# Column mixing moved off the tensor engine, and a last batch in another order, in a decoder layer's attention stage

## The reference

```python
# attention: A has one value for each batch and column
Xn = layernorm(X) * gamma + beta
Q, K, V = split(Xn @ W_in + b_in, 3)
K, V = rotary(K, 256), rotary(V, 256)      # columns 2n and 2n+1 turn together
A = sum over tokens of (K / |K|) * (V / |V|)
A = 0.5 * A + 0.5
x1 = layernorm(X + (X + (A * Q) @ W_out + b_out))
# cross product: both sides rounded to an fp8 grid, scale = 448 / max|t| over the whole tensor
x2 = layernorm(x1 + q8(x1) @ q8(ctx) + mask)
# feed-forward: silu(x2 @ gate) * (x2 @ up) @ down, and 8 retrieved experts a token
out = layernorm(x2 + ffn(x2))
```

## Time and profile before

| | before |
|---|---|
| three runs | 790.91 us median (790.62 to 791.0) |
| the profiled execution: time, span | 791.2 us, 789.4 us |
| PE busy (share of the span) | 775.0 us (98%) |
| DVE | 664.5 us (84%) |
| POOL (GpSimd) | 360.5 us (46%) |
| ACT (ScalarE) | 322.0 us (41%) |
| mean granted TensorE clock | 0.997 |
| accumulating transfers `total<-prod` (384 KB) | 11, median 4.1 us to landing |
| accumulating transfers `xall<-half_bo` (1 MB) | 4, median 9.2 us to landing |

### The profile page before, as it was taken

The page is one execution under the profiler, slowest core; times in us unless marked ns, Lnnn a source line. Parts: engine busy times, 40 slices in busy tenths (PEclk is TensorE's granted clock), DMA queues, the critical chain, the costliest instruction groups (busy, mean ns, idle before and its releaser), DMA issues.

```text
span 789.4 us, 10701 instructions
## 1 busy us (share of the span) xinstructions
PE 775.0 (98%) x3586; PEld 637.9 (81%) x3590; DVE 664.5 (84%) x1348; ACT 322.0 (41%) x704; POOL 360.5 (46%) x313
## 2 busy tenths in 40 slices
PE   8999999999899999999999999999999999999997
PEld 7888888887678778888888888888888888888885
DVE  6888679998898871476779998999999999899876
ACT  5454336456574422223443433343333343344324
POOL 1241222232122411014476676775776677676324
PEclk9999999999999999999999999999999999999999
DMA  8656504624455629001122221331233323242014
GB/s 318 252 128 167 94 0 101 174 76 75 76 142 117 149 90 295 1 1 32 50 77 81 83 88 41 118 104 47 86 113 110 92 79 113 63 128 62 16 54 159
DMA packets 51334, 79.92 MB, mean 101 GB/s; under 512 B 17519, under 2 KB 26479, under 8 KB 50768
## 3 DMA queue, kind: packets, MB, share of 16 engines
q0 software_dynamic: 24240, 31.52, 19.1%
q1 hardware_dynamic: 25456, 47.72, 17.4%
q10 hardware_dynamic: 1584, 0.01, 0.1%
HBM read 110.64 MB, written 12.58 MB: 156 GB/s over the span
## 4 chain that ended last, share of the span: by engine, by line
PE 65%; DVE 3%; issue 2%; POOL 2%; ACT 1%; POOLq 0%; ACTq 0%; DVEq 0%
PE gu L1883 14%; PE gu L1884 14%; PE gu L1885 14%; PE ob L1957 6%; PE ob L1956 6%; PE ob L1961 6%; PE ob L1910 1%; POOL h_lo L1311 1%; DVE scratch L1575 1%; DVE x_lo L1622 1%; DVE scratch L1577 0%; PE gu L2055 0%; DVE xall L1616 0%; PE ob L1977 0%; POOL xall L153 0%
## 5 line engine op out<-in xcount | busy, mean ns | idle before, releaser
L1883 PE MATMUL gu<-x_hi,w_hi 128*128 128x512 f32 x516 | 201.4, 390 | 0.0
L1885 PE MATMUL gu<-x_hi,w_lo 128*128 128x512 f32 x516 | 200.8, 389 | 0.0
L1884 PE MATMUL gu<-x_lo,w_hi 128*128 128x512 f32 x516 | 200.7, 389 | 0.0
L1311 POOL TENSOR_TENSOR h_lo<-mid,h_hi 128x512 fp32r<-128x512 f32 x62 | 86.8, 1417 | 175.4 <-ACT h_hi L1461 175.4
L1885 PEld LDWEIGHTS gu<-x_hi,w_lo 128*128 128x128 f32 x516 | 96.8, 188 | 20.2
L1883 PEld LDWEIGHTS gu<-x_hi,w_hi 128*128 128x128 f32 x516 | 96.9, 188 | 20.0
L1884 PEld LDWEIGHTS gu<-x_lo,w_hi 128*128 128x128 f32 x516 | 96.9, 188 | 19.9
L1471 ACT ACTIVATE gates<-dots 128x1 f32<-128x1 f32 x144 | 29.2, 203 | 175.2 <-DVE dots L1724 175.2
L1633 DVE TENSOR_TENSOR mid<-gu,mid 128x512 f32<-128x512 f32 x64 | 44.0, 687 | 64.1 <-PE gu L1885 54.2
L1956 PE MATMUL ob<-w_hi,h_hi 128*128 128x512 f32 x224 | 87.1, 389 | 0.0
L1957 PE MATMUL ob<-w_lo,h_hi 128*128 128x512 f32 x224 | 87.1, 389 | 0.0
(11 more groups left out here) (254 smaller groups left out, 1438.1 us busy)
## 6 DMA issues: line engine op xcount, KB each, us to landing
stage<-in_ctx SPq DMA_DIRECT2D x7, 1024.0 KB, 5.8
total<-prod POOLq DMA_DIRECT2D x11, 384.0 KB, 4.1
xall<-half_bo POOLq DMA_DIRECT2D x4, 1024.0 KB, 9.2
xhat<-in_L_ffn_gate_w SPq DMA_DIRECT2D x8, 512.0 KB, 3.5
xhat<-in_L_ffn_up_w SPq DMA_DIRECT2D x8, 512.0 KB, 3.8
xall<-in_mask_Bx1xS_ff POOLq DMA_DIRECT2D x4, 1024.0 KB, 11.0
xhat<-in_L_ffn_down_w SPq DMA_DIRECT2D x8, 512.0 KB, 3.6
x_dram<-xall SPq DMA_DIRECT2D x4, 1024.0 KB, 7.8
```

The costliest lines, as they stand in the source:

```text
L1311: nc.gpsimd.tensor_tensor(lo[:, c], mid[c][:], hi[:, c].bitcast(F32), ALU.subtract).then_inc(hlo_done, 1)
L1883: nc.tensor.matmul(dst, lhs[0], rhs[0], start=start, stop=False)
L1884: nc.tensor.matmul(dst, lhs[0], rhs[1], start=False, stop=False)
L1885: return nc.tensor.matmul(dst, lhs[1], rhs[0], start=False, stop=stop)
```

## The change

1. **Mixing.** The products with `mix`, ScalarE's copy and the matrix itself are gone. The rotary columns of `total` are joined before the token sums, by three instructions of 128 x 256: on GpSimd for batches 0 to 2 (`mix_total`), on DVE for the last (in `last_total`). PE then sums four chunks, and `total` has two buffers, taken in turn.
2. **ctx.** The scale is made at the end of batch 1, and each rounding stands one place earlier: batch 3's in batch 2's first half, batch 0's at its end, batch 1's at the start of batch 3, batch 2's in its middle.
3. **Last batch.** All token sums stand together ahead of the last step of the third query chunk. The attention's first tile takes three chunks of y, then the fourth. The transposes of x1 stand behind the attention, and 16 idle products are gone.
4. **Variance.** For the last batch's tiles 0 to 2 DVE's residual also gives the row sums; ScalarE centres and squares, GpSimd makes the variance and the power. Batch 2's x1 is normalised by one ScalarE instruction a tile instead of two.
5. **Mask.** Batch 0's mask is added in two transfers of half the size, issued behind the last power.
6. **`low_ffn`** is on GpSimd, right behind the last bias transfer.

```diff
@@ GpSimd
-                    nc.gpsimd.dma_start(total[:], prod[:, i % 2], accum_op=ALU.add).then_inc(total_in, 16)
+                    nc.gpsimd.dma_start(totals[b % 2][:], prod[:, i % 2], accum_op=ALU.add).then_inc(total_in, 16)
+
+                def mix_total(b):
+
+                    pool.wait_ge(total_in, 16 * 3 * (b + 1))
+                    plain, turned = totals[b % 2][:, 0:ROT], totals[b % 2][:, D:D + ROT]
+                    apart = prod[:, 0, 0:ROT]
+                    own.did(nc.gpsimd.tensor_tensor(apart, plain, turned, ALU.subtract))
+                    own.did(nc.gpsimd.tensor_tensor(plain, plain, turned, ALU.add))
+                    own.wait()
+                    nc.gpsimd.tensor_tensor(plain.rearrange("p (n t) -> p n t", t=2), plain.rearrange("p (n t) -> p n t", t=2),
+                                            apart.rearrange("p (n t) -> p n t", t=2)[:, :, ::-1], ALU.add).then_inc(total_mixed, 1)
...
+                def low_ffn(s, part):
+                    pool.wait_ge(whi_done, s + 1)
+                    nc.gpsimd.tensor_tensor(part[1], w_stage[s].rearrange("p (c n) -> p c n", c=KC), part[0].bitcast(F32), ALU.subtract).then_inc(wlo_done, 1)
+
+                def last_rstd(i):
+
+                    pool.wait_ge(x1_scaled, i + 1)
+                    pool.wait_ge(last_squared, i + 1)
+                    own.did(nc.gpsimd.tensor_scalar(var2[:, i:i + 1], last_square[:, i:i + 1], 1.0 / D, LN_EPS, ALU.mult, ALU.add))
+                    own.wait()
+                    last_z_rstd(slice(i, i + 1))
+
+                for s, part in enumerate((gate_s[0], up_s[0])):
+                    low_ffn(s, part)
...
-                add_mask(0)
...
+                pool.wait_ge(x1_scaled, TB)
+                pool.wait_ge(var2_ready, LAST + 1)
+                last_z_rstd(slice(TB - 1, TB))
+                add_first_mask()
@@ ScalarE
-                def copy_sums(b):
...
+                def square_last(i):
+                    act.wait_ge(x1_centred, i + 1)
+                    if i:
+                        act.wait_ge(last_squared, i)
+                    nc.scalar.activation(junk[:], tile(TB * LAST + i), ACT.Square, accum_out=last_square[:, i:i + 1]).then_inc(last_squared, 1)
@@ DVE
-                    nc.vector.tensor_tensor(total[:], total[:], prod[:, (TB - 1) % 2], ALU.add).then_inc(total_all, 1)
+                    total = totals[LAST % 2]
+                    own.did(nc.vector.tensor_tensor(total[:], total[:], prod[:, (TB - 1) % 2], ALU.add))
+                    own.wait()
+                    plain, turned = total[:, 0:ROT], total[:, D:D + ROT]
+                    dve.wait_ge(total_mixed, LAST)
+                    apart = crossed[:]
+                    own.did(nc.vector.tensor_tensor(apart, plain, turned, ALU.subtract))
+                    own.did(nc.vector.tensor_tensor(plain, plain, turned, ALU.add))
+                    own.wait()
...
-                    if b == LAST:
-                        ctx_quantise(2)
+                    if b == LAST:
+                        ctx_quantise(3)
...
-                for s, part in enumerate((gate_s[0], up_s[0])):
-                    low_ffn(s, part)
@@ PE
-                        last = nc.tensor.matmul(ob[0][:, c:c + 1], total[:, c * P:(c + 1) * P], ones_col[:], start=(c == 0), stop=(c == CHUNKS - 1), skip_group_check=True)
+                        halved = 0 if c * P < ROT else 1
+                        last = nc.tensor.matmul(ob[0][:, c:c + 1], totals[b % 2][:, c * P:(c + 1) * P], sum_cols[:, halved:halved + 1], start=(c == 0), stop=(c == KC - 1), skip_group_check=True)
-                def mix_sums(b):
...
-                        for k in range(KC):
-                            pe.wait_ge(yhi_done, KC * b + k + 1)
...
+                        for chunks in (range(KC),) if b < LAST else (range(KC - 1), (KC - 1,)):
+                            for k in chunks:
+                                pe.wait_ge(yhi_done, KC * b + k + 1)
```

More of the change, by code:

```diff
@@ L132, in decoder_layer @@
         amax1 = keep("amax1", [P, 2], F32)
+        last_stats = keep("last_stats", [P, 4, TB], F32)
+        last_sum, last_minus, last_square, shift2 = (last_stats[:, i] for i in range(4))
         arow = keep("arow", [1, 4], F32)
@@ L154, in add_mask, with add_first_mask @@
                                 accum_op=ALU.add).then_inc(xm_in[b], 16)
+        def add_first_mask():
+            nc.gpsimd.wait_ge(x1t_mm, TB)
+            for first, landed in ((0, xm_in[0]), (2, xm_late)):
+                nc.gpsimd.dma_start(xall[:, first * D:(first + 2) * D].rearrange("p (t n) -> p t n", t=2), mask[0, 0].partition_broadcast(P).unsqueeze(1).broadcast_to([P, 2, D]),
+                                    accum_op=ALU.add).then_inc(landed, 16)
         s_const, ident_in = sem("s_const"), sem("ident_in")
@@ L177, in decoder_layer @@
             kv = sb("kv", [P, 2, 2, D], F32)
-            total = sb("total", [P, D + ROT], F32)
+            totals = [sb(f"total{i}", [P, D + ROT], F32) for i in range(2)]
             prod = sb("prod", [P, 2, D + ROT], F32)
@@ L364, in _ @@
                 last_z_rstd(slice(0, TB))
-                add_mask(0)
[L366 to L371, removed]
+                pool.wait_ge(minus_ready, 1)
+                pool.wait_ge(rstd2_ready, LAST)
+                nc.gpsimd.tensor_tensor(shift2, minus_m2[:], rstd2[:], ALU.mult).then_inc(shift_ready, 1)
+                for i in range(TB - 1):
+                    last_rstd(i)
+                pool.wait_ge(x1_scaled, TB)
+                pool.wait_ge(var2_ready, LAST + 1)
+                last_z_rstd(slice(TB - 1, TB))
+                add_first_mask()
+                first_psteps.append(own.base + own.n)
             @block.scalar
@@ L646, in products @@
                     k_t, v_t, w_t = kv[:, i % 2, 0], kv[:, i % 2, 1], wgt[:, i % 2]
-                    into = prod[:, i % 2] if i else total
+                    into = prod[:, i % 2] if i else totals[b % 2]
                     both, rotated, sinp = into[:, 0:D], into[:, D:D + ROT], crossed[:]
@@ L811, in _ @@
                     if b:
-                        for i in range(1, TB):
-                            residual(b - 1, i)
+                        residual(b - 1, 1)
+                        if b == 1:
+                            ctx_amax(3)
+                            dve.wait_ge(c_amax, B)
+                            largest(amax_c[:])
+                        residual(b - 1, 2)
+                        residual(b - 1, 3)
+                        if b == 1:
+                            scale_row()
                         variance(range(TB))
-                    if b == 1:
-                        ctx_amax(3)
-                        dve.wait_ge(c_amax, B)
-                        largest(amax_c[:])
+                        if b == 1:
+                            scale_all()
                 residual(LAST - 1, 0)
@@ L963, in query @@
                     for k in range(KC):
-                        if sums is not None and k:
-                            token_sums(sums, range(2 * k - 2, 2 * k))
-                        if mix_of is not None and k == 1:
-                            mix_sums(mix_of)
+                        if sums is not None and k == KC - 1:
+                            token_sums(sums, range(KC))
                         last = three(ob[2 + c % 2][:], w_hi[:, k, c * P:(c + 1) * P], w_lo[:, k, c * P:(c + 1) * P], xn_hi[:, k], xn_lo[:, k], k == 0, k == KC - 1)
@@ L1067, in _ @@
                 query(LAST, 2, sums=LAST)
-                query(LAST, 3, mix_of=LAST)
+                query(LAST, 3)
+                for i in range(TB):
+                    attention(LAST, i)
                 pe.wait_ge(x1_done, TB)
@@ L1074, in _ @@
                     last.then_inc(x1t_mm, 1)
-                for i in range(TB):
-                    attention(LAST, i)
                 def keep_running(count):
```

227 lines of the change are left out of this document (107 added, 120 removed).

## The result

The changed kernel takes 805.0 us (median of 4 runs, 804.6 to 805.9) against 790.95 us (4 runs, 790.62 to 791.53): a ratio of 1.0177 with a 95% interval of 1.0166 to 1.0189, so it is 14.1 us slower, where 792.9 (788.0 to 795.3) was forecast.

A forecast was written before the change was run, and what follows sets the result against it. PE was taken to set the time up to 205.0 us, DVE from there. Attention +1.0, tail -0.6 and clock +1.6 gave +2.0 on the median of 790.91: 792.9, range 788.0 to 795.3.

The forecast's parts named there:

- The mask: Start of the next stage: mask halves landing 6 and 11 to 12 us after issue cost 0, bounds 0 and 2.
- The rival about the mask: Next stage: the second mask half lands late, the third tile waits up to 2 us: 794.9; chance 0.14.
- The clock: Behind PE's 5.3 us stop before the last token sums: 3.4 us at 1.2 GHz, 1.7 lost at most, 1.6 taken.
- The first rival: PE's clock stays full through the stop before the last token sums: +0.4, 791.3; chance 0.28.
- The lower halves: Last batch's last products: GpSimd's two subtractions hold DVE for two turns, 4.7 us lost, bounds 0 and 4.8.
- A miss: GpSimd's subtractions hold DVE's last products once or not at all: 788.9 or 786.6; chance 0.16.
- Last batch: Mixed `total` ready at 190.8, not 183.98; then 15.1 us instead of 20.9; attention ends at 206.0, 1.0 late.
- The tail's gain of 0.6: Behind the attention: only one maximum, not two, stands behind the last tile's shift: -0.6.
- Sums and rounding: Batches 0 to 2: cheaper sums and mixing save PE 3.0 us; waits from batch 2's earlier rounding give it back.
- the offset of 0.85: End of batch 2: DVE is about 0.9 late, so PE ends about 0.85 late; bounds 0.3 and 1.5.
- the step that put the mixing on GpSimd at nothing: Batches 0 to 2: three GpSimd operations, estimated 0.65 us each, replace PE's mixing at cost 0, bounds 0 and 2.
- the reason given (ScalarE's row): Batch 2: `amul` 1.05 later, ScalarE's unbroken row delivers the first query at 124.1 instead of 123.05; PE waits 2 us.

The follow-up runs named there:

- the run with the pair behind y: The changed kernel without GpSimd's drain, the lower halves of the first feed-forward weights left on GpSimd but behind the last y: 788.4 us.

## Why the prediction was wrong, point by point

**The mask.** The step "the first half is needed some 10 us later ... 0, bounds 0 and 2" failed, and with it the forecast. Its landing times were near enough: 6 and 11 to 12 us behind the first issue were forecast, about 7 and 11 measured. What the step asked was when the mask is used, and not what else waits for its landing: GpSimd's drain at the end of the part. That cost 8.2 in the trace; 8.0 by the run without the drain, 8.5 by the mask alone moved in the kernel before. The row was there to be read: before, the drain was 1.5 us long, and the mask had been issued at 194.7, 12 us ahead of it. The rival about the mask had the right transfer and the wrong waiter.

**The clock.** The step had the stop right (5.3, measured 5.50) and its price too small: "1.7 us lost at most" took the 3.4 us at half clock behind the one fall in the earlier trace rows for the most that a fall can cost. Here 7.3 us of work ran at half, which is 3.7; the run with the stop filled gave back 3.3. In the kernel before with the lower halves on GpSimd it was 6.8 us of work, behind a stop of 2.26. So one fall is no bound for another; what sets the length is open. The first rival (the clock holds) was wrong.

**The lower halves.** Right in mechanism, place and sign, and the step on which the stop rests. The size was 5.4 instead of 4.7: DVE did not get one instruction in between GpSimd's two, as the turns in the earlier trace rows had suggested, but stood for both. That the first product and not the third was held follows from the starts in the records: GpSimd's pair was put 2.5 us behind the start of the bias transfer's issue (1.63 and 0.85), and its record begins 0.80 behind it (178.54 against 177.74), while that issue and DVE's products had moved together, by 1.1. A miss was possible, as the prediction allowed: in the kernel before, the same pair cost 2.3 to 8.5 us from run to run.

**Last batch.** Mixed total at 191.75 instead of 190.8; without the clock, the 18.85 us from the token sums to the end of the attention are 15.1, as worked out. The tail's gain of 0.6 came and was lost again (5.95 against 5.99). Up to the last maximum it is 0.5 shorter, and behind it DVE's diagonal instruction (`junk<-ident,amax`), 0.29 before, took 0.71 while GpSimd issued the mask; it took 0.29 again in the run that issues the mask in the next part. This cost of the mask's place had no term either.

**Sums and rounding.** 2.5 us were saved and lost in batch 2 by the wait that was named, at 2.20 us for 2; the offset of 0.85 at the end of batch 2 was 0.81. By the last products it was 1.1: the step that put the mixing on GpSimd at nothing left out that its operations, too, meet DVE instructions with two operands from SBUF. At the start of batch 3 one rounding took 2.71 instead of 2.29, and the last of the three mixing operations 2.75, where the first two took 0.74 and 0.73. But the wait was only the first of DVE's: the reason given (ScalarE's row) was true and did not carry, since with ScalarE out of the way the residual took the wait over. That DVE sets the pace there is shown by the runs; that it is the 4.6 us of the rounding which came into this stretch is read from the order and was not run alone.

**Sum.** +1.0 in the attention was +2.0 (0.7 of it by the longer hold, 0.3 by DVE's offset), the clock's 1.6 was 3.7, -0.6 was 0.0, and 8.2 had no term: 13.9.

## What to carry to other kernels

A transfer that is moved later has two deadlines, its first reader and every drain or barrier that it is moved towards; look up the barrier's row before costing the move at nothing. Work that is moved from DVE to GpSimd was free here beside residuals and maxima, which read one operand from SBUF, and was paid in full beside products, which read two, so its price is set by the instruction it lands on. One operand is no safe sign by itself: the diagonal instruction has one tensor operand, and lost 0.4 beside the issue of a transfer. When a wait is removed and the time stays, look which engine the next wait names; take work from that engine in the stretch where it has no pause, and nowhere else. A clock price that is read from one fall is a sample, not a bound.

## What the runs showed of the hardware that was not expected

- GpSimd's drain at the end of a part lasted until its own transfers had landed: 11.0 and 11.6 us right behind mask transfers, 1.5 us where the transfer had landed before and 2.0 where none was out.
- Two GpSimd subtractions of 128x1024 issued one behind the other held a DVE instruction with two SBUF operands for both of their lengths (6.13 us instead of 0.73, in three traces), with no turn between; where they met the fifth product instruction it was held for one of them (2.51 instead of 0.42).
- A stop of 5.5 us cost 3.7 us more behind it, as the clock came back only after 7.3 us of work; identity products of 128x128 through the stop kept it at 2.4 GHz. A stop of 2.2 us in batch 2 left it at 1.00 in this trace; the same stop in the run with the pair behind y was followed by 0.83 over 126 to 134.
